# Two normalise-and-add passes folded into the attention and feed-forward stages of a four-stage layer kernel

## What is computed

```
x = x + layernorm(attention(layernorm(x)))      # 16 heads of width 8, latent keys and values
x = x + layernorm(feedforward(layernorm(x)))    # silu(x Wg) * (x Wu), then Wd; hidden width 384
x = x + layernorm(statespace_mlp(layernorm(x)))
x = x + layernorm(experts(layernorm(x)))
```

## Time and profile before

| what | us |
|---|---|
| median of 3 runs | 1483.64 |
| lowest and highest run | 1483.19, 1488.87 |
| the profiled execution, whole | 1490.55 |
| its span, first to last instruction | 1488.8 |
| start of pass r1, of feed-forward, of state space in it | 636.6, 671.7, 843.3 |

### The profile page before, as it was taken

One profiled execution on the slowest core, in us unless ns is written; L12 is line 12 of the kernel. 1 busy time (PEld: TensorE's weight loads), 2 busy tenths in 40 slices (PEclk: granted clock), 3 DMA queues, 4 the chain that ended last, 5 costly groups with the idle time before them and its releaser, 6 DMA issues. The chain is left out here.

```text
span 1488.8 us, 26460 instructions
## 1 busy us (share of the span) xinstructions
PE 1200.2 (81%) x7410; PEld 535.8 (36%) x7458; DVE 914.6 (61%) x2719; ACT 923.7 (62%) x1379; POOL 514.8 (35%) x757
## 2 busy tenths in 40 slices
PE   3689999999999999807996057599759999999983
PEld 1122222222222222204664057377523433334431
DVE  3487666666776766575776866543345656657552
ACT  2588989998999999753344371233424665555553
POOL 5333333333344441051112700000052555655534
PEclk7799999999999999957998578799969999999997
DMA  4665555565555454009500011000000000000000
GB/s 122 124 116 102 96 105 102 106 111 106 102 102 102 96 101 95 1 17 213 180 0 1 28 58 57 1 0 0 0 1 1 8 8 14 14 7 14 15 15 22
DMA packets 71171, 87.89 MB, mean 59 GB/s; under 512 B 10136, under 2 KB 64958, under 8 KB 65214
## 3 DMA queue, kind: packets, MB, share of 16 engines
q1 hardware_dynamic: 69078, 85.55, 27.4%
q10 hardware_dynamic: 2024, 1.51, 0.4%
HBM read 63.84 MB, written 31.59 MB: 64 GB/s over the span
## 5 line engine op out<-in xcount | busy, mean ns | idle before, releaser
L454 ACT ACTIVATE a_probs<-a_S 128x1024 f32<-128x1024 f32 x512 | 495.6, 1036 | 80.4 <-DVE a_S L596 75.3
L596 DVE TENSOR_TENSOR a_S<-a_S,a_tables 128x256 f32<-128x256 f32 (+1 forms) x512 | 281.4, 561 | 186.1 <-PE a_S L470 183.3
L477 PE MATMUL a_O<-a_probs,a_V 128*32 128x512 f32 x2048 | 275.4, 610 | 2.4 <-ACT a_probs L454 0.6
L470 PE MATMUL a_S<-a_Qs,a_Ks 48*128 48x512 bf16 x1024 | 180.0, 389 | 27.7 <-DMA a_Qs<-a_parts_dram 15.5
L470 PEld LDWEIGHTS a_S<-a_Qs,a_Ks 48*128 48x128 bf16 x1024 | 42.7, 93 | 243.3 <-ACT a_probs L454 195.2
L384 POOL CAST a_parts<-a_whole 128x512 bf16<-128x512 f32 x47 | 29.1, 620 | 275.3 <-DVE a_whole L606 264.9
L1976 ACT ACTIVATE e_hid<-e_H 128x512 f32<-128x512 f32 x128 | 69.5, 594 | 83.6 <-PE e_H L2081 83.6
L1729 ACT ACTIVATE g_hid<-g_H,w_b 128x512 f32<-128x512 f32 x64 | 44.0, 687 | 87.1 <-PE g_H L1750 87.1
L2079 PE MATMUL e_H<-e_gated,w_We 64*128 64x512 f32 x256 | 75.9, 670 | 13.3 <-DVE e_gated L2179 11.4
L1207 POOL TENSOR_TENSOR XY<-XY x32 | 40.4, 1264 | 108.8 <-ACT XY L1224 99.9
L2090 PE MATMUL e_O<-e_hid,w_We 128*64 128x512 f32 x256 | 74.3, 630 | 2.3 <-issue 1.8
(11 more groups left out here) (318 smaller groups left out, 2248.5 us busy)
## 6 DMA issues: line engine op xcount, KB each, us to landing
a_parts_dram<-a_parts SPq DMA_DIRECT2D x94, 192.0 KB, 5.6
a_Qs<-a_parts_dram SPq DMA_DIRECT2D x64, 192.0 KB
a_Qs<-a_parts_dram SPq DMA_DIRECT2D x64, 128.0 KB
m_taps_by_step<-h_taps SPq DMA_DIRECT2D x8, 1024.0 KB, 13.3
m_taps<-m_taps_by_step SPq DMA_DIRECT2D x8, 1024.0 KB, 5.2
a_Ks<-a_parts_dram SPq DMA_DIRECT2D x30, 192.0 KB
XY<-L_attn_x SPq DMA_DIRECT2D x16, 256.0 KB, 6.8
a_Qs<-a_parts_dram SPq DMA_DIRECT2D x64, 64.0 KB
```

The costliest lines, as they stand in the source:

```text
L454: act.activation(probs[n % KEPT][:], S[n % RING][:], ACT.Exp).then_inc(exped, 1)
L470: mm = pe.matmul(S[n % RING][:, par, :], Ks[p][rows, pr, kb * P:(kb + 1) * P], Qs[p][Q_OF(kb)][rows, pr, :], start=True, stop=True)
L477: mm = pe.matmul(O[VC * j:VC * (j + 1), :], V[q][:, kb, HG * g + j, :], probs[(2 * m + j // 2) % KEPT][:, j % 2, :], start=(kb == 0), stop ...
L596: v.tensor_tensor(s[:, :, where], s[:, :, where], wide, ALU.mult).then_inc(corrected, 1)
```

## The change

Both passes are gone. What they did is done in the blocks ahead.

In attention, batch t-2 is finished during batch t: VectorE computes its output moments after tile 11; GpSimd, at the head of its turn for batch t, inverts the root and does three wide operations (`add_to`: plus the negated mean, times the inverse root, add to x); VectorE waits for that after tile 21 and takes the statistics of the new x, and their moments after tile 24; GpSimd inverts that root at the end of its turn. GpSimd's layer norm for a batch to come moves from the head of its turn to the end of the turn before. Batch 14 is finished at the end of the block and batch 15 at the start of feed-forward. The input's mean and inverse root get arrays of their own.

In feed-forward, batch t-2's statistics and moments are taken in turn t, and batch t-3 is normalised by ScalarE, straight from the `f_OUT` bank, in pieces of 128 columns; VectorE's copy is gone. GpSimd adds to x, VectorE takes statistics of the batch four back. After the last batch comes a tail for the last four batches and the moments and roots of all. The guarded attention loads x anew and has a pass of its own (`rejoin_guarded`), which isn't run here; `check_range` uses one semaphore for four.

Cut to what matters:

```diff
+    def add_to(self, pool, u, p):
+        Y, X = self.core.Y[:, u + 1], self.core.X[:, u]
...
+        self.invert(pool, u, self.rstd, p)
+        pool.tensor_tensor(Y, Y, wide(self.neg), ALU.add).then_inc(self.inverted, 1)
+        settled(1)
+        pool.tensor_tensor(Y, Y, wide(self.rstd), ALU.mult).then_inc(self.inverted, 1)
+        settled(2)
+        pool.tensor_tensor(X, X, Y, ALU.add).then_inc(self.inverted, 1)
+    def wait_added(self, eng, u):
+        eng.wait_ge(self.inverted, u * (self.INVERT + self.ADD) + (self.INVERT + self.ADD))
...
             def body(t, p, first=False, ahead=True, more=True, fresh=True):
+                if not isinstance(t, int) or t >= 2:
+                    out_norm.add_to(pool, t - 2, p)
                 if not ahead:
+                    if not more:
+                        out_norm.add_to(pool, t - 1, 1 - p)
+                    next_norm.invert(pool, t - 2, core.xrstd, p)
+                    if not more:
+                        next_norm.invert(pool, t - 1, core.xrstd, 1 - p)
                     return
-                second = isinstance(t, int) and t == 1
-                pool.wait_ge(m_full, FIRST["xT1"] if first else use(t - 1, "xT", second))
-                pool.sem_inc(core.turns, 1)
-                layer_norm(t + 2)
                 for w, name in enumerate("qqk"):
                     lower(t + 2, w, use(t, name, first))
                 if not isinstance(t, int) or t < B - 3:
-                    joined.invert(pool, t + 3, core.xrstd)
+                    joined.invert(pool, t + 3, core.in_rstd, 1 - p)
+                    pool.wait_ge(m_full, use(t, "xT", first))
+                    pool.sem_inc(core.turns, 1)
+                    layer_norm(t + 3)
+                if not isinstance(t, int) or t >= 2:
+                    next_norm.invert(pool, t - 2, core.xrstd, p)
...
+                    if n == 15 and not more:
+                        out_norm.moments_of(v, t - 1, None, p=1 - p)
+                    if n == 11 and (not isinstance(t, int) or t >= 2):
+                        out_norm.moments_of(v, t - 2, None, p=p)
+                    if n == 21 and (not isinstance(t, int) or t >= 2):
+                        out_norm.wait_added(v, t - 2)
+                        next_norm.moments_of(v, t - 2, X[:, t - 2], only_stats=True, p=p)
+                    if n == 24 and (not isinstance(t, int) or t >= 2):
+                        next_norm.moments_of(v, t - 2, None, core.xmean, p=p)
...
             batches(v, body)
+            out_norm.wait_added(v, B - 2)
+            next_norm.moments_of(v, B - 2, X[:, B - 2], core.xmean, p=0)
...
@@ swiglu, GpSimd
+            core.out_norm.add_to(pool, B - 1, 1)
+            core.next_norm.invert(pool, B - 1, core.xrstd, 1)
...
+            out.constant(pool, init, 1)
             trailing(0, 0)
+            def invert(b):
+                out.invert(pool, b, out.rstd)
+                out.offset(pool, b)
+            def add(b, q, n):
+                OUT[q].after(pool, n)
+                pool.sem_inc(core.turns, 1)
+                pool.tensor_tensor(X[:, b], X[:, b], Y[:, b + 1], ALU.add).then_inc(added, 1)
             def body(t, p, i):
                 if comes(t, 1):
                     trailing(t + 1, 1 - p)
+                if started(t, 3):
+                    add(t - 3, 1 - p, i if p else i - 1)
+                if started(t, 2):
+                    invert(t - 2)
             batches(pool, body)
+            add(B - 3, 1, B // 2 - 1)
+            invert(B - 2)
+            invert(B - 1)
+            for b in (B - 2, B - 1):
+                add(b, b % 2, B // 2)
@@ swiglu, ScalarE
+            def normalise(b, q, half):
+                if half == 0:
+                    out.wait(act, b)
+                for c in range(half * NT // 2, (half + 1) * NT // 2):
+                    op = act.activation(Y[:, b + 1, c], OUT[q].t[:, tile_of(core, c)], ACT.Identity,
+                                        bias=out.offsets[:, b, c:c + 1], scale=out.rstd[:, b, c:c + 1])
+                if half:
+                    OUT[q].emptied(op)
...
                 for m in range(FC):
                     if m == 1 and comes(t, 1):
                         middle(t + 1, 1 - p)
+                    if m and started(t, 3):
+                        normalise(t - 3, 1 - p, m - 1)
...
+            act.preload_act_table(ACT.Sqrt)
+            for b in range(B - 3, B):
+                for half in range(2):
+                    normalise(b, b % 2, half)
+            act.wait_ge(steps, ROOTS)
+            act.activation(roots[:], roots[:], ACT.Sqrt).then_inc(rooted, 1)
@@ swiglu, VectorE
             v.sem_inc(hid_done, 2)
+            core.out_norm.moments_of(v, B - 1, None, p=1)
...
             layer_norm(1)
+            core.out_norm.wait_added(v, B - 1)
+            core.next_norm.moments_of(v, B - 1, X[:, B - 1], core.xmean, p=1)
...
             def body(t, p, i):
+                if started(t, 2):
+                    out_statistics(t - 2, p, i)
                 if comes(t, 1):
                     remainder(t + 1, 1 - p)
...
+                hidden(t, p, 0)
+                if started(t, 2):
+                    out.moments_of(v, t - 2, None)
+                hidden(t, p, 1)
                 if comes(t, 2):
+                    v.wait_ge(core.next_norm.inverted, B * Norm.INVERT)
                     layer_norm(t + 2)
-                take_out(t - 1, 1 - p, i + 1)
+                hidden(t, p, 2)
+                if started(t, 4):
+                    statistics(t - 4)
...
@@ program
-            add_normed(core, "r1")
             swiglu(core, I, W, taps)
             ints_ctx.close()
-            add_normed(core, "r2", rms=True)
             state_space(core, I, flt, taps)
```

More of the change, by code:

```diff
@@ L987, in _ @@
             sp.dma_start(decay[:], I["decay"]).then_inc(const, 16)
-            sp.wait_ge(const, 16)
+            for b in range(B):
+                sp.dma_start(X[:, b], xv[:, b]).then_inc(const, 16)
+            sp.wait_ge(const, LOADED)
             with sp.Fori(0, B) as t:
@@ L1491, in take_out, with statistics @@
                 for c in range(NT):
                     op = v.bn_stats(core.yst[:, b + 1, c], OUT[q].t[:, tile_of(core, c)])
[L1493 removed]
+                op.then_inc(out.steps, 1)
+            def statistics(b):
+                v.wait_ge(added, b + 1)
+                for c in range(NT):
+                    op = v.bn_stats(core.xst[:, b, c], X[:, b, c])
+                op.then_inc(counted, 1)
             v.wait_ge(init, 1)
             batches(v, body)
[L1497 removed]
+            for b in (B - 2, B - 1):
+                out_statistics(b, b % 2, B // 2)
+                out.moments_of(v, b, None)
@@ new lines, in _ @@
+            for b in range(B - 4, B):
+                statistics(b)
+            v.wait_ge(counted, B)
+            tick = Tally(v, steps)
+            moments(v, tick, core.xst[:], core.xmean[:, 0:B], var[:], mean[:])
+            tick.mark(v.tensor_scalar(roots[:, 0], var[:], 1e-5, None, ALU.add))
+            tick.mark(v.tensor_scalar(roots[:, 1], var[:], 1.0 + 1e-6, 1e-11, ALU.mult, ALU.add))
+            assert tick.n == ROOTS
+            v.wait_ge(rooted, 1)
+            tick.mark(v.reciprocal(core.xrstd[:, 0:B], roots[:, 0]))
@@ L1500 @@
+            tick.step(v.reciprocal(core.urstd[:, 0:B], roots[:, 1]))
 class Taps:
@@ L2270, in program @@
         flt = Filter(core, I)
+        core.out_norm = Norm(core, ctx, "after", core.yst[:, 1:B + 1], affine=False, deep=2, after=Norm.ADD)
+        core.next_norm = Norm(core, ctx, "next", core.xst, affine=False, deep=2)
         attention(core, I, flt)
```

305 lines of the change are left out of this document (122 added, 183 removed).

## The result

The changed kernel took 1439.57 us, median of four runs (1435.92 to 1442.80), against 1486.26 us (1483.19 to 1491.14) before on the same chip: a ratio of 0.968, 95% interval 0.9647 to 0.9714. That is 46.7 us or 3.2% less. The prediction was 36.6 us less, 1447.0, with a range of 1437 to 1459. The time lies inside it, but 10 us of gain came unforecast.

The account below looks back on a forecast made before the run. Adding passes were bound by VectorE and GpSimd waiting for each other, feed-forward by TensorE, attention by a ring of engines. 35.1 + 22.1 - 1.4 - 7.0 - 12.2 = 36.6 us off 1483.64 gave 1447.0, range 1437 to 1459.

Parts of the forecast that it names:

- The first pass: Adding pass between attention and feed-forward: its block goes, so feed-forward begins 35.1 us earlier.
- Work inside attention: Attention, batches 0 to 13: the first pass's work fits mostly into VectorE's holes, costing 1.4 us, bounds 0 and 7.
- the charge of 0.1 a batch: Attention after tile 21: the statistics make the next correction 0.4 late, charged at 0.1 us a batch, 1.4 in all.
- the slack that I had worked out: Attention after tile 21: GpSimd finishes the addition to x 2.9 us before VectorE asks, so no wait.
- C: Attention has no real holes: 0.5 us a batch, 7 in place of 1.4, 1452.6 us; chance 0.10.
- D: Attention: VectorE stops after tile 21 because GpSimd isn't done, slower than before, 1504 us; chance 0.03.
- The shared port: VectorE and GpSimd: certain VectorE operations are held until a wide GpSimd operation ends, such as 1.18 us on 32 columns.
- The Trainium skill's warning that the prediction cites: GpSimd and VectorE share an SBUF read port, so moving operations between them might not help; spoke against the change.
- The head: Start of feed-forward: batch 15's work delays the first trailing third from 12.0 to 19.0 us, costing 7.0, bounds 5.5 and 8.
- The loop: Feed-forward batches: TensorE's bank wait gives 8.05 us, VectorE's loop 8.0; 8.3 taken in place of 7.3, costing 12.2.
- rival A: Feed-forward loop: ScalarE's pieces are short and little is held, period 7.6 us, 1438.6 us in all; chance 0.15.
- The tail: End of feed-forward to the state space stage, without the second pass: gain 22.1 us, bounds 19 and 24.

Follow-up runs that it names:

- e7: Kernel before the change, with only attention's input layer norm moved to the end of GpSimd's turn; 1487.32 us, ratio 0.9999.
- e4: Changed kernel with VectorE reordered in the feed-forward loop: output statistics and moments before the second hidden product, statistics of x before the layer norm; 1437.65 us.
- e12: Changed kernel with attention's input layer norm put back at the start of GpSimd's turn; 1447.59 us, ratio 0.9741.
- e2: Changed kernel, but in feed-forward ScalarE copies the output in one piece instead of four normalising pieces, leaving out the norm for batches 0 to 12; 1432.14 us.
- e1: Changed kernel without VectorE's statistics of x in the feed-forward loop; 1439.70 us.
- e3: Changed kernel, but at the head of feed-forward GpSimd makes the first trailing third before batch 15's root; 1433.04 us, ratio 0.9617.
- e5: Changed kernel with the feed-forward loop reordered: GpSimd's root before its addition, ScalarE's pairs one product piece earlier, output statistics beside the trailing third; 1437.36 us.

## Why the prediction was right, and where it was not

- **The first pass** (35.1): right. Its block is gone whole.
- **Work inside attention** (-1.4 forecast, +5.6 found, of which 4.1 are the change's): the step that failed. The groups after tiles 11, 21 and 24 are in holes, as said: from the 12th exponential to the end of the batch, where the second and third stand, the changed kernel is within 0.04 us of e7 over all batches, and in the first part, where the first group stands, it is no longer than e7 either; so the charge of 0.1 a batch measured 0. The addition to x was done 2.9 us ahead of the statistics after tile 21 (it ends at 324.31, they begin at 327.24), the slack that I had worked out; rivals C and D did not come. What I left out is two other edits of the change. One is a move: the input layer norm goes from the start of a turn to the end of the one before (1.8 us of held checks, 1.4 of them by this move alone in e7). I had the rule of the held operations, even noted 328.4 beside 328.57, and used it only against the change. I did not ask which VectorE operations the layer norm of the kernel before already held. The rows for it were in the trace. The other is the helper's two places by parity, which the prediction doesn't mention (2.3 us, by the traces). The 1.5 left are no miss of mine: they are the clock in batch 3 of the trace of before.
- **The shared port**: right, in every place. Held were operations on two SBUF inputs (0.16 to 0.92 and 1.05) and the scaled copies of the layer norm (1.11 to 2.19); statistics on one input kept 0.22 each beside the addition in e4. The Trainium skill (SBUF — State Buffer, Who interferes with whom) says that an operation of VectorE on two SBUF inputs contends with one of GpSimd that reads SBUF, and of the shared port pair that whoever issues first gets it for the whole instruction and the other blocks, and the rows agree: 0.90 in place of 0.21 behind a layer norm that began 0.22 earlier. The Trainium skill's warning that the prediction cites (Perfetto Trace Analysis, Optimizing Scalar/DVE Operations) held for the loop, with 1.85 us held in a batch. For attention the runs went the other way: there the change set the two engines' operations apart, which brought 1.8 us, and undoing it in e12 cost 7.5.
- **The head** (-7.0 forecast, -8.9 found, bounds 5.5 and 8): mechanism right, a term missing. VectorE's start, 3.3 us after the other engines', had no row in the kernel before: there it was 1.83 us of "issue" into the first pass; it is 4.43 to 4.84 in all eleven kernels whose stage begins like the changed one's, and 1.82 or 1.83 in the three where the first pass follows. I did not settle its cause (see the last section). It was partly paid back, since the casts of the weights took 0.89 in place of 2.25.
- **The loop** (-12.2 forecast, -5.2 found): mechanism right, mis-sized. The waits are the two that I named, and rival A's time (1438.6) was nearer than mine, but by luck: it needed short pieces and little held, and a pair took 0.80 and 1.85 us a batch were held. ScalarE's pieces cost near what I took (a pair 0.80, not 0.87), but four operations in a row overlap: from split to the end of pair two it is 2.5 us, not 2.7. VectorE's loop, where e2 shows it alone, is 7.64, not 8.0. And I added 0.25 us for register instructions to the greater of the two loops with no row for them; e1 has none of it. The period is 0.5 above 7.3, not 1.0.
- **The tail** (22.1 forecast, 23.1 found): right, step by step. Product 15 waits 3.01 us for its bank.
- **The time**: 36.6 forecast, 46.7 found. Of the 10 us, the traces give 7.0 to the loop, 7.2 to attention, 1.0 to the tail, less 1.9 in the head; that is 13.3, and 3 more than the medians say. 1.5 of these 3 are the clock in batch 3 of the trace of before, the rest is less than the runs vary by. That 1439.6 still lay inside the range is partly luck: the two large misses went the same way, and no rival stood for a gain in attention.

## What to carry to other kernels

Before a difference between two traces is given to the change, compare the granted clock of the same stretch: 3.4 us at half clock made 1.5 us here, which look just like a gain of the change. When work moves on GpSimd, list the VectorE operations beside its old place as well as beside the new one: the operations that it stops holding are a gain of the same kind as the loss you are looking for. Where several engines pass buffers round in a loop, the period is at least that of the longest ring. Relieving one ring shows the next (7.84, 7.77, 7.64, here 0.1 apart), and an order that gives one engine air can lengthen another ring (8.02, 8.10). At the head of a stage, put what the bound engine needs ahead of what merely has to be done, and place each wait where its answer has already come.

## What the hardware showed that I had not expected

- After the jump over the guarded code VectorE began 4.43 to 4.84 us after its last operation, with "issue" as the reason, where it had been 1.83 us; GpSimd and ScalarE began 3.3 us earlier than it in the changed kernel. In all eleven traces two packets of 8 KB of the instruction queue q14 landed in between, the second 1.2 to 1.6 us before VectorE began (632.62 and 634.21 in the changed kernel); in the three others VectorE had begun before such packets came (637.16 and 637.85 in the kernel before). That points to a load of instructions, but no run tests it, and why the kernels differ is open.
- The length of attention's batches repeats to 0.1 us over 13 batches (460.02 to 460.14 in ten kernels), while whole runs spread over 4 to 10 us. The two that agree on 465.70 agree by a fall of the clock in each.
- The granted clock falls to half for 3.4 us here and there, in some executions and not in others of the same code, and each fall costs 1.5 to 1.6 us: batch 1 of attention takes 38.96 to 38.98 us in the five traces without one there, 40.45 to 40.55 in the eight with one near 110, and 42.10 in e2, with two. From product 14 to the next stage it is 21.1 us in the changed kernel and 22.7 in e3, which have the same code there; e3 has one more fall, at 770.2. Where such falls are taken out, a trace tells an effect of 1 or 2 us that ten runs can't.
- One of GpSimd's four-column operations (the power, here 1.08 us) beside VectorE's layer norm did not hold it: in e5 the power began at 702.79, the layer norm at 702.98, and its four pieces kept 1.10.
